# One strip loop of a deformable convolution: row terms without a spare pair, masks summed into PSUM, one bias sum for the values

## The chip, the core and the metric

The kernel runs on one core of a Trainium2 chip. The metric is the device time of one execution in microseconds. Before the change it is 2926.32 us, the median of three runs (2924.11 to 2930.4).

## What is computed

The input is 32 samples of 64 channels, 56 x 56. Two residual blocks run one after the other. The first is a pair of binary 3 x 3 group convolutions with batch norms. The second, which the change concerns, is a deformable convolution on the group-normalised sum:

```python
value = (xf @ vp_w.T + vp_b).reshape(n, L, G, cg)          # G = 8 groups of cg = 8 channels
om_in = depthwise_conv3x3(x, dw_w) + dw_b
om = om_in @ om_w.T + om_b                                 # per pixel and group: 18 offsets, 9 masks
py = row + tap_dy + off[..., 0]; px = col + tap_dx + off[..., 1]
sampled = bilinear gather of value at (py, px), zero outside the image
out = einsum('nhwgk,nhwgkc->nhwgc', mask, sampled) @ op_w.T
x = x + out
```

## The kernel before

The first block runs in passes over all samples (`l0_passes`), up to about 700 us. Then `l1_pass` handles the deformable convolution, two samples (a pair) at a time: 16 pairs, each in NT = 14 strips of BR = 4 image rows, so 224 steps. A second general path follows for offsets of a pixel or more; with these inputs it is skipped.

The gather is not done by addresses. Since offsets stay under one pixel, a bilinear sample is a product of two "hat" factors over a 5 x 5 window. For each pixel, group and tap the kernel multiplies the mask by a row hat (`mask_hats`, into `mh`) and by a column hat (`products`, into `pr`), sums the nine taps into a 5 x 5 window of weights (GpSimd `merge`, then TensorE `windows`, which shifts by columns with the matrices `smat`), and writes the weights as a band matrix through a DRAM scratch (`wst`, `w_d`) into `abuf`. TensorE multiplies this band with the values (`vbd`) in `apply`. An `apply` covers two strips (8 rows); its left and right half of the image (34 and 26 columns) go to an even and an odd step.

All engines run their own loop over the steps and meet through semaphores. Let t be the step. What each does in it, in its order:

- VectorE (`step` under `block.vector`): `copy_om(t+2)` (L960) adds the bias to the offsets and masks in PSUM `om_p` and puts them into SBUF `oms`; `mask_hats(t+1)` (L969); three `products(t+1)` (L979); in steps 0, 1, 2, 3, 5, 6 one `sum_half` and in step 7 two and the channel statistics of the next pair (L920 to L937); then `read_misc(t)`, which waits for TensorE and does `add_output` (L986) and `copy_values` (L952), in step 8 after the group statistics (L940 to L945).
- GpSimd: `merge(t+1)` (L1062, L1065), then `depthwise(t+4)`, four sums that end with L1055 and release the offsets' matmuls.
- ScalarE: `hats(t+2)` (L1119 to L1125), every second step `copy_acc`, `copy_weights(t)` (L1135, four instructions), every second step the DMA of the weights, `taps(t+5)` (L1109).
- TensorE: `apply` of an earlier strip, `windows(t)` (L1258), then one group: value rows (L1195) and offset rows for t+3 (L1200) interleaved, and the projection (L1207), whose last matmul releases `read_misc(t)`. The offset rows overwrite `om_p`, which is there once, so the group first waits for `om_ok` of tile t+2, for `dw_ok` of GpSimd, and for VectorE's last `read_misc`.
- SyncE issues the reads of `abuf` and `vbd` and the images' transfers.

The PSUM is full: `om_p`, `win_p` and `mh_p` have two banks of 512 floats each, `acc_p` and `misc` one. One row of the weights in `abuf` and `wst` has RP = 6 row terms (five and a spare), in the layout two rows x two parts, so the apply at L1280 moves whole pairs of rows (the last index, two neighbours in memory) and covers up to three pairs for each image row.

## Time and profile before

| | us |
|---|---|
| median of three runs | 2926.32 |
| the profiled execution | 2924.83 |
| its span, first to last instruction | 2923.0 |
| busy in the span: PE, DVE, ACT, POOL | 2430.8, 2205.6, 2259.7, 1917.6 |
| mean granted TensorE clock | 0.952 of full |

PE is TensorE, DVE VectorE, ACT ScalarE, POOL GpSimd; L960 is line 960. A busy time says only that an engine had an instruction running. The chain of waits of this page ends in the short flag test behind the loop and does not tell of the steps, so the reading goes by stretches, by the order of instructions in time, and by the waits.

### The profile page before, as it was taken

How to read it: one execution, taken by the hardware profiler on the slowest of the kernel's cores; microseconds unless marked ns; L12 is line 12 of the kernel's file. 1: busy time of each engine (PE TensorE's matmuls, PEld its weight loads, DVE VectorE, ACT ScalarE, POOL GpSimd, SP SyncE). 2: the span in 40 equal slices, each digit the busy share in tenths (PEclk: the TensorE clock that was granted, in tenths of full speed). 3: DMA queues.
4: the chain of work that ended last, by engine and by line, in shares of the span. 5: the costliest groups of instructions: out<-in, count | busy, mean ns of one | idle time of the engine just before them, and what ended most of it. 6: DMA issues, size and time to landing. Idle time of an engine off the chain costs nothing. (4 is left out here: it accounts for less than half of the span.)

```text
span 2923.0 us, 100581 instructions
## 1 busy us (share of the span) xinstructions
PE 2430.8 (83%) x40456; PEld 2021.2 (69%) x40456; DVE 2205.6 (75%) x3095; ACT 2259.7 (77%) x4721; POOL 1917.6 (66%) x1452
## 2 busy tenths in 40 slices
PE   3999779993688888888888888888888888888887
PEld 2666556772577777777777777777777777777786
DVE  3555423334989897989888898989898988989773
ACT  2444256662989889898989898898989898989892
POOL 1000000003888888888988888888988898988892
PEclk8999889996899999999999999999999999999998
DMA  4555579975577677777777777777778777877675
GB/s 103 130 132 144 143 182 265 263 199 172 124 191 203 181 195 192 188 191 190 204 194 192 187 200 195 197 183 193 199 189 198 188 196 187 206 179 190 177 176 147
DMA packets 356164, 538.18 MB, mean 184 GB/s; under 512 B 171728, under 2 KB 258256, under 8 KB 355536
## 3 DMA queue, kind: packets, MB, share of 16 engines
q1 hardware_dynamic: 296656, 422.71, 60.3%
q10 hardware_dynamic: 59136, 110.11, 10.8%
q8 instruction: 283, 4.64, 0.8%
q14 instruction: 89, 0.73, 0.1%
HBM read 312.82 MB, written 219.77 MB: 182 GB/s over the span
## 5 line engine op out<-in xcount | busy, mean ns | idle before, releaser
L1109 ACT ACTIVATE dwt<-xp,wts 128x224 f32<-128x224 f32 x2016 | 797.3, 484 | 40.8 <-ACT wst L1135 31.8
L1280 PE MATMUL acc_p<-abuf,vbd 128*32 128x136 f32 (+5 forms) x20480 | 710.4, 291 | 54.9 <-issue 46.0
L1280 PEld LDWEIGHTS acc_p<-abuf,vbd 128*32 128x32 f32 (+1 forms) x20480 | 645.9, 145 | 117.7 <-issue 60.5
L979 DVE TENSOR_TENSOR pr<-mh_p,ht 128x864 f32<-128x864 f32 x672 | 668.9, 1051 | 23.2
L1258 PE MATMUL win_p<-pr,smat 128*128 128x160 f32 x4032 | 626.7, 310 | 27.3 <-POOL pr L1065 15.8
L246 PE MATMUL cv<-cin,wb 128*64 128x392 bf16 x6912 | 590.4, 333 | 25.8 <-ACT cin L225 25.8
L1258 PEld LDWEIGHTS win_p<-pr,smat 128*128 128x128 f32 x4032 | 570.4, 194 | 51.2 <-issue 22.4
L246 PEld LDWEIGHTS cv<-cin,wb 128*64 128x64 bf16 x6912 | 401.4, 110 | 208.7 <-ACT cin L225 25.9
L1048 POOL TENSOR_TENSOR dwt<-dwt 128x896 f32<-128x896 f32 x224 | 516.3, 2305 | 4.7 <-ACT dwt L1109 4.7
L1062 POOL TENSOR_TENSOR pr<-pr 128x576 f32<-128x576 f32 x224 | 317.3, 1417 | 187.8 <-DVE pr L979 187.8
L1135 ACT ACTIVATE wst<-win_p 128x200 f32<-128x200 f32 x896 | 388.6, 605 | 62.4 <-PE win_p L1258 38.7
L969 DVE TENSOR_TENSOR mh_p<-oms,ht 128x864 f32<-128x864 f32 x224 | 408.8, 1825 | 8.5 <-ACT ht L1125 8.5
L1200 PE MATMUL om_p<-wts,omin 64*64 64x216 f32 x3584 | 406.4, 369 | 10.2 <-POOL omin L1055 10.2
L1195 PE MATMUL misc<-wts,xp 64*64 64x64 f32 x3584 | 181.6, 234 | 265.7 <-issue 214.3
L1195 PEld LDWEIGHTS misc<-wts,xp 64*64 64x64 f32 x3584 | 149.8, 137 | 311.2 <-issue 310.7
L1065 POOL TENSOR_TENSOR pr<-pr 128x576 f32<-128x576 f32 x224 | 338.7, 1512 | 31.2
L1050 POOL TENSOR_TENSOR dwt<-dwt 128x448 f32<-128x448 f32 x224 | 336.5, 1502 | 17.6
L1200 PEld LDWEIGHTS om_p<-wts,omin 64*64 64x64 f32 x3584 | 246.1, 139 | 47.8 <-issue 11.6
L986 DVE TENSOR_TENSOR y<-y,misc 128x224 f32 (+1 forms) x224 | 85.2, 380 | 248.2 <-PE misc L1207 247.5
L253 ACT ACTIVATE lt<-cv 128x392 f32<-128x392 f32 x128 | 60.9, 492 | 265.9 <-PE cv L246 265.5
L960 DVE TENSOR_TENSOR oms<-om_p,ombt 128x864 f32<-128x864 f32 x224 | 238.2, 1063 | 10.1 <-PE om_p L1200 10.1
L1119 ACT ACTIVATE ht<-oms 128x576 f32<-128x576 f32 x224 | 151.2, 675 | 102.7 <-DVE oms L960 102.4
(132 smaller groups left out, 2674.9 us busy)
## 6 DMA issues: line engine op xcount, KB each, us to landing
abuf<-weight_scratch SPq DMA_DIRECT2D x1568, 96.0 KB, 3.3
weight_scratch<-wst ACTq DMA_DIRECT2D x112, 960.0 KB, 6.2
xt<-x SPq DMA_DIRECT2D x128, 392.0 KB, 7.6
rows_scratch<-vsb SPq DMA_DIRECT2D x224, 128.0 KB, 2.1
vbd<-rows_scratch SPq DMA_DIRECT2D x896, 32.0 KB, 3.2
x_scratch<-xt SPq DMA_DIRECT2D x64, 392.0 KB, 6.6
y<-x SPq DMA_DIRECT2D x64, 392.0 KB, 4.4
x3h<-x_scratch SPq DMA_DIRECT2D x64, 392.0 KB, 4.9
```

Source lines behind the costliest of these rows:

```text
L246: mm = pe.matmul(cv[c][64 * h:64 * h + 64, 0:CN], wb[:, layer, j, k, :], cin[:, u, r:r + CR, k % 3:k % 3 + W], start=(k == 0 and j == 0), ...
L969: dve.tensor_tensor(mh[:, :, :, :], oms[:, j % 2, 2 * TAPS:3 * TAPS, :].unsqueeze(1).broadcast_to([LANES, 3, TAPS, BR * G]), ht[:, j % 2, ...
L979: dve.tensor_tensor(pr[:, j % 2, slots, :, :, :].rearrange("p k e x z -> p e k (x z)"), mh[:, a, :, :].rearrange("p (k x) z -> p k (x z)", ...
L1048: pool.tensor_tensor(d[:, 0:4, :], d[:, 0:4, :], d[:, 4:8, :], ALU.add).then_inc(dw1_ok, 1)
L1050: pool.tensor_tensor(d[:, 0:2, :], d[:, 0:2, :], d[:, 2:4, :], ALU.add).then_inc(dw2_ok, 1)
L1065: pool.tensor_tensor(rows(slice(1, 3)), rows(slice(1, 3)), rows(slice(5, 11, 5)), ALU.add).then_inc(mg_ok, 1)
L1109: ins = act.activation(dwt[:, j % 2, k, :].rearrange("p (r w) -> p r w", w=W), image[:, r:r + BR, k % 3:k % 3 + W], ACT.Identity, scale=dw ...
L1135: ins = act.activation(bass.AP(cells.tensor, cells.offset, [cells.ap[0], [PC, CT], [2 * BR, 2 * RT], [BAND, GS]]), win_p[:, 0:CT * WP].rea ...
L1195: return pe.matmul(misc[64 - 64 * s:128 - 64 * s, to:to + C], xp[64 * s:64 * s + 64, at:at + XL], vpw[64 * s:64 * s + 64, :], start=True, ...
L1200: return pe.matmul(om_p[64 * s:64 * s + 64, 256 * r:256 * r + OMC], omin[64 * s:64 * s + 64, j % 2, r, :], omw[64 * s:64 * s + 64, :], sta ...
L1258: mm = pe.matmul(win_p[:, to:to + 160], smat[:, e, :], pr[:, j % 2, 0:RT, a, b, :], start=n == 0, stop=n == len(terms) - 1)
L1280: mm = pe.matmul(acc_p[32 * (2 * s + b):32 * (2 * s + b) + 32, 0:2 * TN].rearrange("p (t w r) -> p t w r", t=BR, r=2)[:, t0:t1 + 1, x0:x1, :],
```

## The change

There are five parts.

1. The spare row term goes: a cell has RT = 5 rows of RW = 16 weights (PC 96 to 80 floats, a band 480 to 416 with a tail of 16, a line's read 768 to 656). The apply can then no longer move whole pairs everywhere: where a range of rows begins with an odd or ends with an even row, that row gets a matmul of its own with one element per column instead of two. A full strip goes from 12 matmuls over 48 rows to 18 over 40 for each of the four column groups.
2. The windows lie without gaps in `win_p`, so the fourth of them crosses from one bank to the next, and its matmuls are cut in two (11 instead of 9 a step, two records each).
3. `copy_weights` takes two ScalarE instructions of 400 elements instead of four of 200.
4. `copy_om` is split. `copy_offsets` writes 576 elements to `oms` in its old place. `copy_masks` writes 288 masks into the middle slot of `mh`, which lies in PSUM and is free only when the products of the tile before are done, so it stands behind the products, and `om_ok` is set there. `mask_hats` then reads its masks from PSUM: first the two outer hats (576 elements), then the middle one in place (288).
5. The values' bias is added by one instruction of 256 elements instead of two of 128; its constant is loaded once instead of twice.

```diff
@@ -58,15 +58,14 @@
 GS = 4
 CT = 5
 RT = 5
-RP = RT + 1
-WP = 172
-PC = 2 * BR * RP * 2
-BAND = CT * PC
+RW = 4 * BR
+PC = RT * RW
+BAND = CT * PC + RW
 PX = 4
-SEEN = (PX + CT - 1) * PC
+SEEN = (PX - 1) * PC + BAND
 LINE = GS * SEEN + PC
-QB = 36
-QC = 64
+QB = 37
+QC = 65
 VSLOT = 7
 TP = 2 * W
 TILES = HW // TP
@@ -947,28 +945,35 @@
                 def copy_values(i, j):
                     u = j % 2
                     wait(dve, v_out[u], 16 * turn(i, j))
-                    for h in range(2):
-                        at = TN + 2 * C * h
-                        ins = dve.tensor_tensor(
-                            vsb[:, u, :, :, 4 * h:4 * h + 4].rearrange("p g c a -> p a g c"),
-                            misc[:, at:at + 2 * C].rearrange("p (a g c) -> p a g c", g=GS, c=G),
-                            vbt[:, :, :].rearrange("p k (b g c) -> p (k b) g c", g=GS, c=G), ALU.add)
-                    return ins
-
-                def copy_om(i, j):
+                    return dve.tensor_tensor(
+                        vsb[:, u, :, :, :].rearrange("p g c (k b) -> p k b g c", b=2),
+                        misc[:, TN:TN + BR * C].rearrange("p (k b g c) -> p k b g c", k=BR, b=2, g=GS),
+                        vbt[:, :].rearrange("p (b g c) -> p b g c", b=2, g=GS).unsqueeze(1).broadcast_to([LANES, BR, 2, GS, G]), ALU.add)
+
+                def offset_sums(i, j, to, lo, hi):
+                    return dve.tensor_tensor(
+                        to.rearrange("q w (g k) -> q (w g) k", k=BR),
+                        om_p[:, :].rearrange("q (k z) -> q z k", k=BR)[:, G * lo:G * hi, :],
+                        ombt[:, G * lo:G * hi].unsqueeze(2).broadcast_to([LANES, G * (hi - lo), BR]), ALU.add)
+
+                def copy_offsets(i, j):
                     dve.wait_ge(om_ready, NT * i + j + 1)
-                    dve.tensor_tensor(
-                        oms[:, j % 2, :, :].rearrange("q w (b k g) -> q (w b) k g", b=2, g=GS),
-                        om_p[:, :].rearrange("q (k z) -> q k z", k=BR)[:, :, 0:OMC].rearrange("q k (v g) -> q v k g", g=GS),
-                        ombt[:, :].rearrange("q (v g) -> q v g", g=GS).unsqueeze(2).broadcast_to([LANES, 6 * TAPS, BR, GS]),
-                        ALU.add).then_inc(om_ok, 1)
+                    offset_sums(i, j, oms[:, j % 2, :, :], 0, 2 * TAPS).then_inc(off_ok, 1)
+
+                def copy_masks(i, j):
+                    t = NT * i + j
+                    dve.wait_ge(om_ready, t + 1)
+                    wait(dve, pr_ok, 3 * t)
+                    offset_sums(i, j, mh[:, 1, :, :], 2 * TAPS, 3 * TAPS).then_inc(om_ok, 1)
 
                 def mask_hats(i, j):
-                    wait(dve, pr_ok, 3 * (NT * i + j))
-                    dve.wait_ge(hat_ok, NT * i + j + 1)
-                    dve.tensor_tensor(mh[:, :, :, :],
-                                      oms[:, j % 2, 2 * TAPS:3 * TAPS, :].unsqueeze(1).broadcast_to([LANES, 3, TAPS, BR * G]),
-                                      ht[:, j % 2, :, 0:TAPS, :], ALU.mult).then_inc(mh_ok, 1)
+                    t = NT * i + j
+                    dve.wait_ge(om_ok, t + 1)
+                    dve.wait_ge(hat_ok, t + 1)
+                    dve.tensor_tensor(mh[:, 0:3:2, :, :], mh[:, 1, :, :].unsqueeze(1).broadcast_to([LANES, 2, TAPS, BR * G]),
+                                      ht[:, j % 2, 0:3:2, 0:TAPS, :], ALU.mult).then_inc(outer_ok, 1)
+                    dve.wait_ge(outer_ok, t + 1)
+                    dve.tensor_tensor(mh[:, 1, :, :], mh[:, 1, :, :], ht[:, j % 2, 1, 0:TAPS, :], ALU.mult).then_inc(mh_ok, 1)
 
                 def products(i, j):
 
@@ -998,11 +1003,14 @@
                 def step(i, j, first, last):
                     n = near(i, j, 2, first, last)
                     if n:
-                        copy_om(*n)
+                        copy_offsets(*n)
                     n = near(i, j, 1, first, last)
                     if n:
                         mask_hats(*n)
                         products(*n)
+                    n = near(i, j, 2, first, last)
+                    if n:
+                        copy_masks(*n)
...
@@ -1017,10 +1025,12 @@
...
                 for j in range(2):
...
-                for j in range(2):
-                    copy_om(0, j)
+                copy_offsets(0, 0)
+                copy_masks(0, 0)
+                copy_offsets(0, 1)
                 mask_hats(0, 0)
                 products(0, 0)
+                copy_masks(0, 1)
...
                     step(0, j, True, False)
...
@@ -1113,9 +1123,9 @@
 
                 def hats(i, j):
                     t, u = NT * i + j, j % 2
-                    off = oms[:, u, 0:2 * TAPS, :]
+                    off = oms[:, u, :, :]
                     wait(act, pr_ok, 3 * (t - 1))
-                    act.wait_ge(om_ok, t + 1)
+                    act.wait_ge(off_ok, t + 1)
...
                     act.wait_ge(abs_ok, t + 1)
@@ -1129,13 +1139,12 @@
                     if u == 0:
                         wait(act, w_out, 16 * (t // 2))
                     act.wait_ge(win_ok, t + 1)
-                    for k in range(BR):
-                        to = 2 * BR * (2 - 2 * (k % 2)) + BR * u + k
+                    for r in range(2):
+                        to = RW * (1 - r) + BR * u + r
                         cells = wst[:, 0, to:to + 1]
                         ins = act.activation(
-                            bass.AP(cells.tensor, cells.offset, [cells.ap[0], [PC, CT], [2 * BR, 2 * RT], [BAND, GS]]),
-                            win_p[:, 0:CT * WP].rearrange("p (e z) -> p e z", e=CT)[:, :, 0:RT * BR * G].rearrange(
-                                "p e (m k g) -> p e m k g", k=BR, g=GS)[:, :, :, k, :],
+                            bass.AP(cells.tensor, cells.offset, [cells.ap[0], [2 * BR, 2 * CT * RT], [BAND, GS], [2, 2]]),
+                            win_p[:, 0:CT * RT * BR * G].rearrange("p (m g k r) -> p r m g k", g=GS, k=2, r=2)[:, r],
                             ACT.Copy)
                     ins.then_inc(wst_ok, 1)
 
@@ -1253,11 +1262,12 @@
                     pe.wait_ge(mg_ok, t + 1)
                     for e in range(CT):
                         terms = [(a, b) for a in range(3) for b in range(3) if 2 - (a + b - 2) == e]
-                        to = WP * e
+                        cuts = (0, 1, RT) if e == 3 else (0, RT)
                         for n, (a, b) in enumerate(terms):
-                            mm = pe.matmul(win_p[:, to:to + 160], smat[:, e, :],
-                                           pr[:, j % 2, 0:RT, a, b, :],
-                                           start=n == 0, stop=n == len(terms) - 1)
+                            for m0, m1 in zip(cuts, cuts[1:]):
+                                mm = pe.matmul(win_p[:, BR * G * (RT * e + m0):BR * G * (RT * e + m1)], smat[:, e, :],
+                                               pr[:, j % 2, m0:m1, a, b, :],
+                                               start=n == 0, stop=n == len(terms) - 1)
                     mm.then_inc(win_ok, 1)
 
                 def apply(i, j, half):
@@ -1271,17 +1281,24 @@
                     qb, K, x0, x1 = ((0, 128, 0, 34), (1, 96, 30, W))[half]
                     rows = range(max(0, y0 - 2), min(H, y0 + 2 * BR + 2))
                     for yq in rows:
-                        t0, t1 = max(0, yq - y0 - 2) // 2, min(2 * BR - 1, yq - y0 + 2) // 2
-                        for s in range(S):
-                            for b in range(2):
-                                seen = abuf[0:K, s, :]
-                                at = (QB * qb + x0 - 32 * qb + 2) * PC + 4 * BR * (y0 + 2 * t0 - yq + 3) + 2 * BR * b + 2 * t0
-                                mov = bass.AP(seen.tensor, seen.offset + at, [seen.ap[0], [8 * BR + 2, t1 - t0 + 1], [PC, x1 - x0], [1, 2]])
-                                mm = pe.matmul(
-                                    acc_p[32 * (2 * s + b):32 * (2 * s + b) + 32, 0:2 * TN].rearrange("p (t w r) -> p t w r", t=BR, r=2)[:, t0:t1 + 1, x0:x1, :],
-                                    vbd[0:K, 1 - s, qb, yq // BR % VSLOT, :, :, 2 * (yq % BR) + b].rearrange("p g c -> p (g c)"),
-                                    mov, start=yq == rows[0] and qb == 0, stop=yq == rows[-1] and qb == 1,
-                                    skip_group_check=True)
+                        k0, k1 = max(0, yq - y0 - 2), min(2 * BR - 1, yq - y0 + 2)
+                        t0, t1 = (k0 + 1) // 2, (k1 + 1) // 2
+                        runs = (((k0, 1, 1),) if k0 % 2 else ()) + (((2 * t0, t1 - t0, 2),) if t1 > t0 else ()) + (
+                            ((k1, 1, 1),) if k1 % 2 == 0 else ())
+                        for ka, n, r in runs:
+                            opens = qb == 0 and yq == rows[0] and ka == k0
+                            for s in range(S):
+                                for b in range(2):
+                                    seen = abuf[0:K, s, :]
+                                    row = y0 + ka - yq + 3 - ka % 2
+                                    at = (QB * qb + x0 - 32 * qb + 2) * PC + RW * row + 2 * BR * b + ka
+                                    mov = bass.AP(seen.tensor, seen.offset + at, [seen.ap[0], [2 * RW + 2, n], [PC, x1 - x0], [1, r]])
+                                    mm = pe.matmul(
+                                        acc_p[32 * (2 * s + b):32 * (2 * s + b) + 32, 0:2 * TN].rearrange("p (t w r) -> p t w r", t=BR, r=2)[
+                                            :, ka // 2:ka // 2 + n, x0:x1, ka % 2:ka % 2 + r],
+                                        vbd[0:K, 1 - s, qb, yq // BR % VSLOT, :, :, 2 * (yq % BR) + b].rearrange("p g c -> p (g c)"),
+                                        mov, start=opens, stop=yq == rows[-1] and qb == 1 and ka == runs[-1][0],
+                                        skip_group_check=True)
                     mm.then_inc(amat_ok, 1)
 
                 def step(i, j, first, last):
```

Left out: the declarations of the buffers and semaphores, and the constant's single load.

## Rows read from the trace of the kernel before

**Rows 1.** Stretches: start:end, length, busy (instructions) per engine, clock, DMA share, GB/s
```profile
0.00:700.00 700.00, 596.66 (x6950) 408.05 (x6950) 301.30 (x662) 312.58 (x289) 39.52 (x60) 0.95 0.66 172
...
1500.00:2000.00 500.00, 417.30 (x7812) 367.39 (x7812) 446.40 (x563) 453.26 (x1033) 438.94 (x326) 0.98 0.75 194
```

**Rows 2.** Timeline of VectorE, L960 of one pair: start us, us, instruction
```profile
1548.98 1.07 DVE L960 TENSOR_TENSOR oms<-om_p,ombt 128x864 f32<-128x864 f32 x1
...
1588.35 1.05 DVE L960 TENSOR_TENSOR oms<-om_p,ombt 128x864 f32<-128x864 f32 x1
...
1595.77 1.05 DVE L960 TENSOR_TENSOR oms<-om_p,ombt 128x864 f32<-128x864 f32 x1
...
1616.76 1.05 DVE L960 TENSOR_TENSOR oms<-om_p,ombt 128x864 f32<-128x864 f32 x1
...
1631.54 1.04 DVE L960 TENSOR_TENSOR oms<-om_p,ombt 128x864 f32<-128x864 f32 x1
...
1638.13 1.06 DVE L960 TENSOR_TENSOR oms<-om_p,ombt 128x864 f32<-128x864 f32 x1
...
1682.94 1.07 DVE L960 TENSOR_TENSOR oms<-om_p,ombt 128x864 f32<-128x864 f32 x1
```

**Rows 3.** Timeline of VectorE, a step without a sum; brackets: idle before, releaser
```profile
1656.41 0.39 DVE L986 TENSOR_TENSOR y<-y,misc 128x224 f32 x1 [1.94 <-PE misc L1207]
...
1657.23 1.07 DVE L960 TENSOR_TENSOR oms<-om_p,ombt 128x864 f32<-128x864 f32 x1
1658.20 1.73 DVE L969 TENSOR_TENSOR mh_p<-oms,ht 128x864 f32<-128x864 f32 x1
1660.04 2.99 DVE L979 TENSOR_TENSOR pr<-mh_p,ht 128x864 f32<-128x864 f32 x3
```

**Rows 4.** Timeline of VectorE, step 6 with one sum
```profile
1606.82 1.10 DVE L960 TENSOR_TENSOR oms<-om_p,ombt 128x864 f32<-128x864 f32 x1
...
1612.64 1.03 DVE L920 SCALAR_TENSOR_TENSOR y<-y,ab,x3h 128x392 f32 x1
...
1616.01 0.37 DVE L986 TENSOR_TENSOR y<-y,misc 128x224 f32 x1
```

**Rows 5.** Groups of VectorE, 1000 to 2800: count | busy us, mean ns | idle before
```profile
L979 DVE TENSOR_TENSOR pr<-mh_p,ht 128x864 f32<-128x864 f32 x561 | 558.4, 1051 | 19.5
L969 DVE TENSOR_TENSOR mh_p<-oms,ht 128x864 f32<-128x864 f32 x186 | 342.2, 1840 | 0.0
```

**Rows 6.** Timeline of GpSimd, the last sum of a depthwise
```profile
1653.26 0.67 POOL L1055 TENSOR_TENSOR omin<-dwt 128x224 f32<-128x224 f32 x1
```

**Rows 7.** Timeline of TensorE, an even step's apply and windows, later an odd step
```profile
1511.27 3.42 PE L1280 MATMUL acc_p<-abuf,vbd 128*32 128x68 f32 x96
1514.62 2.71 PE L1258 MATMUL win_p<-pr,smat 128*128 128x160 f32 x18
...
1654.14 0.27 PE L1195 MATMUL misc<-wts,xp 64*64 64x64 f32 x2 [0.57 <-issue]
...
1655.67 0.59 PE L1207 MATMUL misc<-accs,wts 64*64 64x112 f32 x8
1656.19 2.80 PE L1280 MATMUL acc_p<-abuf,vbd 96*32 96x52 f32 x96
```

**Rows 8.** TensorE's waits of the whole run (us, times, longest), and an instruction queue
```profile
PE acc_p L1280 <- issue: 46.0, 41, 3.2
PE win_p L1258 <- issue: 10.7, 11, 2.2
PE acc_p L1280 <- DMA abuf<-weight_scratch: 8.6, 4, 4.4
...
q8 instruction: 283, 4.64, 0.8%
```

**Rows 9.** Timeline of a step 8: the projection, and the add that it releases
```profile
1500.46 0.69 PE L1207 MATMUL misc<-accs,wts 64*64 64x112 f32 x8
...
1502.01 0.37 DVE L986 TENSOR_TENSOR y<-y,misc 128x224 f32 x1
```

More of the change, by code:

```diff
@@ L99, in __init__ @@
         self.ombt = sb("ombt", [LANES, OMC])
[L100 removed]
+        self.vbt = sb("vbt", [LANES, C])
         self.smat = sb("smat", [128, CT, 128])
@@ L117, in load_constants @@
         sp.dma_start(self.ombt[:, :], self.omb_d).then_inc(self.con_in, 16)
-        for k in range(2):
-            sp.dma_start(self.vbt[:, k, :], self.vpb).then_inc(self.con_in, 16)
+        sp.dma_start(self.vbt[:, :], self.vpb).then_inc(self.con_in, 16)
     def clear(self, pool):
@@ L789, in l1_pass @@
         tap_ok, dw1_ok, dw2_ok, dw3_ok, dw_ok = map(sem, ("tap_ok", "dw1_ok", "dw2_ok", "dw3_ok", "dw_ok"))
-        om_ready, om_ok, abs_ok, far_ok, hat_ok, mh_ok, pr_ok, mg1_ok, mg_ok = map(sem, (
-            "om_ready", "om_ok", "abs_ok", "far_ok", "hat_ok", "mh_ok", "pr_ok", "mg1_ok", "mg_ok"))
+        om_ready, off_ok, om_ok, outer_ok, abs_ok, far_ok, hat_ok, mh_ok, pr_ok, mg1_ok, mg_ok = map(sem, (
+            "om_ready", "off_ok", "om_ok", "outer_ok", "abs_ok", "far_ok", "hat_ok", "mh_ok", "pr_ok", "mg1_ok", "mg_ok"))
         win_ok, wst_ok, amat_ok, accs_ok, misc_ready, misc_ok, carried, passed = map(sem, (
```

7 lines of the change are left out of this document (3 added, 4 removed).

## The prediction

> **What bounds the kernel now.** I read the stretch table first [rows 1]. The first 700 us are the convolution block, which the change leaves alone but for one load of constants less. From there to the end runs the second part, 224 strip steps (16 pairs of samples, 14 strips each). In it VectorE, ScalarE, GpSimd and TensorE are each busy 83 to 91% of the time. No engine alone is the bound, and the order of the waits decides.
>
> Second I read VectorE's clock over one pair: the starts of L960, its first instruction of a step, at the steps 0, 4, 5, 7, 8, 9 and the next 0 [rows 2]. Steps 0 to 3 take 39.37 us together, step 4 7.42, steps 5 and 6 20.99, step 7 14.78, step 8 6.59, steps 9 to 13 44.81: 133.96 in all. Steps 0 to 3, 5 and 6 also add one half piece of the input (`sum_half`), step 7 two; there VectorE runs without a stop, step 6 from 1606.82 to 1616.76, 9.94 us [rows 2, 4]. In a step without a sum it waits for TensorE's `misc`, 1.94 us before L986 [rows 3]; TensorE's group in turn starts 0.21 us after GpSimd's L1055 ends (1653.26 + 0.67, then 1654.14) [rows 6, 7]. So VectorE sets the pace of steps 0 to 8, GpSimd through TensorE that of 9 to 13.
>
> Third, TensorE: its offsets-and-misc group takes 2.27 us from the first matmul (1654.14) to the VectorE instruction that it releases (1656.41) [rows 3, 7]. An apply takes 3.42 us for half 0 and 2.80 for half 1, a group of windows 2.71 [rows 7].
>
> **The change, part by part.** *Masks and products on VectorE.* 864 elements with one operand in PSUM take 1.051 us (L979); `mask_hats`, as large, with both in SBUF, 1.840 [rows 5]. The change puts the masks into PSUM. Prices by size: L986 has 224 elements and takes 0.39, L979 1.051, so 1.03 ns an element and 0.16 fixed. L969 starts 0.97 us after L960 [rows 3], so what follows an instruction starts 0.08 + 1.03 ns an element after it. That makes 576 elements 0.67 to the next start and 0.75 in duration, 288 elements 0.37 and 0.45. An instruction that waits for the one before starts 0.11 after its end (L969, 1658.20 + 1.73, to L979, 1660.04) [rows 3].
> No row has a VectorE instruction that steps through PSUM 256 elements at a time, as the two new sums do, or that reads and writes one PSUM tile. Lower bound: these prices, since nothing in such an access saves work. Upper bound: the slowest row of 864 elements, 1.840, so 0.9 ns more an element, and on 1,728 elements 1.6 us a step. I take the lower end, because L960 reads PSUM in jumps already (runs of four) and costs what L979 does.
>
> *Values' bias.* From L986 to L960 pass 0.82 us [rows 3]; L986's own share is 0.30, so the two instructions of 128 elements cost 0.52. One of 256 is 0.34 by size, 0.52 if the store pattern is what costs. I take 0.42.
>
> *The release of `om_p`.* This part decides, I think. `om_ok` lets TensorE overwrite `om_p` with the next offsets. Today L960 sets it, the first work of VectorE's step. Afterwards `copy_masks` sets it, behind the products. Queued behind TensorE's wait are the value rows, the offsets, the projection, and then the next apply and windows; and VectorE's L986 of the same step waits for that projection. So a loop closes in every step: VectorE up to `copy_masks`, TensorE's group, VectorE again. Its length: L986 and the values 0.30 + 0.42; `copy_offsets` 0.67; outer hats 0.75 + 0.11; middle hats 0.45 + 0.11; products 2.99; `copy_masks` 0.11 + 0.45; to TensorE 0.21; the group 2.27. Sum 8.84 us.
> A step with a sum covers TensorE's group: 5.80 to the end of the products, 0.11 + 0.37 until the sum starts, and 3.37 from L920 to L986 (1612.64 to 1616.01) [rows 4]: 9.65 against 9.94.
> Step 8 also has the group statistics: from the projection to L986 1.55 us there, 0.74 elsewhere [rows 3, 7, 9], so 8.84 + 0.81 = 9.65.
> The pair afterwards: steps 0 to 3 38.60; step 4 8.84; steps 5 and 6 19.30; step 7 14.78 - 0.29 = 14.49; step 8 9.65; steps 9 to 13 44.20. Sum 135.08 against 133.96. The steps with sums give back 2.75 us and steps 9 to 13 0.61, but steps 4 and 8 lose 1.42 and 3.06, because today VectorE finds `misc` ready or nearly ready there. Net +1.12 a pair, x16 = +18 us.
>
> *Apply and windows on TensorE.* For each of the four column groups a full strip's apply has 12 matmuls over 48 strip rows, afterwards 18 over 40. A matmul is two records (96 for 48) [rows 7]. The halves have 34 and 26 columns, so 1,632 and 1,248 in all, for 3.42 and 2.80 us: 1.61 ns a column (both records), and 0.79 us remain for 24 passes and the tail. With 0.25 for the tail a pass costs 0.022. Afterwards: 36 x 0.022 + 0.25 + 1,360 or 1,040 x 1.61 ns = 3.23 and 2.72 us. The windows get four records more, each worth between nothing and a whole one of today, 0.15 (2.71 / 18): 0 to 0.6, I take 0.25. TensorE's round from group to group is now 2.05 to the apply (1654.14 to 1656.19), 3.35 to the windows (1511.27 to 1514.62), 2.71 for them: 8.11 with half 0, some 7.5 with half 1. It becomes 8.17 and 7.7, under 8.84 by 0.7 and 1.1.
> That cover is thin, for TensorE also stops in mid-burst for nothing that the profile names: 41 times in applies and 11 times in windows, 56.7 us, 1.1 each [rows 8]. The instruction queue meanwhile moved 283 pieces of 16.4 KB [rows 8]. If the stops are late pieces, they grow with the records: in a step of a full strip 96 in the apply and 58 elsewhere now, 144 and 62 afterwards, and denser. Bounds: no cost, and a whole stop in each of the 112 steps without a sum, 123 us. I take 0.2 us in each: +22 us.
>
> *Parts with one answer.* ScalarE's two copies instead of four come back some tenths of a microsecond, at nothing: in the step shown VectorE waits for TensorE alone [rows 3], and ScalarE works ahead of it. The weights' transfers shrink (rows of 480 to 416 and 768 to 656 elements) with as many issues on ScalarE's and SP's queues as before; the applies behind them waited 8.6 us for them in all [rows 8], so at nothing too.
>
> **Sum.** The profiled execution took 2924.83 us, its span 2923.0 and 1.8 around it; the median of the runs, 2926.32, is 0.05% above, and I correct nothing. 2924.8 + 18 + 22 = 2965 us.
>
> **The rivals.**
> *The loop is shorter than summed (faster).* L920 takes 1.03 us for 392 elements [rows 4], 0.56 by size: it stretches beside GpSimd's merge. Behind `copy_masks` it starts 0.48 later, when that merge is nearly done. If 0.15 us go in each of 8 x 16 sums, that is -19; the values at 0.34 give -18; no late TensorE: 2924.8 + 18 - 37 = 2906. Against: GpSimd only gets its turn later and holds up the next instruction. Chance 0.28.
> *No difference*, within 0.2% (6 us, about what a measurement of this kernel tells from none): half of those gains, 2924. 0.10.
> *The instructions on PSUM cost more.* A quarter of the upper bound, 0.4 us in 224 steps, is +88: 3053. Against: L960's price. 0.10.
> *TensorE becomes the bound.* The new single-row matmuls read one element in every 80, where pairs read two neighbours in every 96. If a column of theirs costs twice, 8 x 34 x 1.61 ns = 0.44 us come on top; with windows at +0.6 the round is 8.96 with half 0, over 8.84, and stops count in full: 0.7 us in 112 steps, +78: 2924.8 + 18 + 78 = 3021. Against: the pairs stream at 0.81 ns a column and record, no worse than the windows' rows without gaps (0.15 / 160, 0.94). 0.12.
> The Trainium skill (SBUF — State Buffer, section "Door 1: The DMA port swizzle", its note on cachelines) says that an access pays when it moves to a new 16-byte line each time, and that two hits a line are wanted. By it the single rows are the bad case and the pairs the good one; this trace has pairs alone, so it does not show the rule either way.
>
> **How the numbers follow.** My case 0.40, at 2965 (2940 to 2990). Faster 0.28, same 0.10, slower 0.40 + 0.10 + 0.12 = 0.62. The range 2895 to 3050 reaches from the faster rival to the two slow ones and leaves out the dearer half of the PSUM bound and a loop still shorter.
>
> **What would show it.** In every step without a sum VectorE should wait some 2.5 us before L986's successor, ended by TensorE, and TensorE's group should be released by `copy_masks` in nearly every step. Steps 4 and 8 should be longer, the steps with sums shorter by about 0.3. The hats should read 0.75 and 0.45 us. Stops within applies should be more numerous. The prediction is wrong if steps 9 to 13 fall well under 8.8 us each, or if TensorE's group is ready by the time that VectorE wants it.

## The result, and the profile after

The changed kernel takes 3102.64 us (median; 3087.4 to 3111.84) against 2925.22 us: ratio 1.060, 95% interval 1.055 to 1.066, so 177 us slower. Slower was forecast, by 40 us; the time lies outside the range given. The profiled execution took 3087.4 us, its span 3085.6.

The first stretch is the same; in the second part VectorE, ScalarE and GpSimd fell from 88 to 91% busy to some 75% [rows 1]. Stretches of the changed kernel (columns as in [rows 1]):

```profile
0.00:700.00 700.00, 597.06 (x6950) 413.89 (x6950) 300.88 (x664) 312.56 (x289) 40.01 (x60) 0.95 0.66 172
1500.00:2000.00 500.00, 414.43 (x9496) 374.50 (x9498) 379.23 (x572) 381.35 (x846) 368.99 (x294) 0.94 0.58 163
```

TensorE has 9,496 matmul records there instead of 7,812 and is no busier; its granted clock is 0.94 instead of 0.98. Groups of VectorE in the changed kernel, 1000 to 2900 us (L948 is the values' bias, L954 the two sums, L973 and L976 the hats, L984 the products):

```profile
L984 DVE TENSOR_TENSOR pr<-mh_p,ht 128x864 f32<-128x864 f32 x546 | 543.7, 1052 | 18.9
...
L954 DVE TENSOR_TENSOR oms<-om_p,ombt 128x576 f32<-128x576 f32 x182 | 141.1, 775 | 0.0
...
L973 DVE TENSOR_TENSOR mh_p<-mh_p,ht 128x576 f32<-128x576 f32 x182 | 136.9, 752 | 0.0
L948 DVE TENSOR_TENSOR vsb<-misc,vbt 128x256 f32<-128x256 f32 x182 | 128.2, 704 | 0.0
...
L976 DVE TENSOR_TENSOR mh_p<-mh_p,ht 128x288 f32<-128x288 f32 x182 | 85.0, 467 | 6.3
L954 DVE TENSOR_TENSOR mh_p<-om_p,ombt 128x288 f32<-128x288 f32 x181 | 84.5, 467 | 6.2
```

VectorE's prices came out as forecast, but for the values' bias: 0.70 us long, and 0.52 to the start of the next instruction (median), where 0.42 was forecast. What grew are the waits. VectorE's wait for `misc` in the kernel before, then waits of the changed kernel, over the whole run (us in all, times, longest):

```profile
DVE y L986 <- PE misc L1207: 247.5, 109, 10.9
```

```profile
DVE y L991 <- PE misc L1216: 479.3, 142, 10.7
...
PE acc_p L1296 <- issue: 217.0, 118, 4.2
...
PE misc L1204 <- DVE mh_p L954: 126.3, 105, 5.1
...
PE win_p L1268 <- issue: 22.3, 17, 3.2
```

and of its page, the queue of instruction pieces:

```profile
q8 instruction: 374, 6.13, 0.8%
```

VectorE waits for `misc` nearly twice as long as before. TensorE's stops in the middle of an apply, which the profile puts down to nothing, went from 46.0 [rows 8] to 217.0 us, and it now waits for `copy_masks` 105 times. Both can be seen in two neighbouring steps. TensorE, changed kernel (start us, us, instruction, in brackets the idle time before):

```profile
1714.33 0.27 PE L1204 MATMUL misc<-wts,xp 64*64 64x64 f32 x2 [1.26 <-DVE mh_p L954]
...
1716.38 2.52 PE L1296 MATMUL acc_p<-abuf,vbd 128*32 128x34 f32 x99
1720.57 1.24 PE L1296 MATMUL acc_p<-abuf,vbd 128*32 128x136 f32 x45 [1.67 <-issue]
1721.74 3.06 PE L1268 MATMUL win_p<-pr,smat 128*128 128x160 f32 x22
1724.73 0.27 PE L1204 MATMUL misc<-wts,xp 64*64 64x64 f32 x2
...
1726.78 2.93 PE L1296 MATMUL acc_p<-abuf,vbd 96*32 96x26 f32 x144
```

and VectorE in the same stretch:

```profile
1716.60 0.39 DVE L991 TENSOR_TENSOR y<-y,misc 128x224 f32 x1 [2.53 <-PE misc L1216]
1716.90 0.73 DVE L948 TENSOR_TENSOR vsb<-misc,vbt 128x256 f32<-128x256 f32 x1
1717.44 0.79 DVE L954 TENSOR_TENSOR oms<-om_p,ombt 128x576 f32<-128x576 f32 x1
...
1719.50 2.99 DVE L984 TENSOR_TENSOR pr<-mh_p,ht 128x864 f32<-128x864 f32 x3
1722.52 0.47 DVE L954 TENSOR_TENSOR mh_p<-om_p,ombt 128x288 f32<-128x288 f32 x1
1727.00 0.39 DVE L991 TENSOR_TENSOR y<-y,misc 128x224 f32 x1 [4.01 <-PE misc L1216]
```

The first group (1714.33) waited for `copy_masks`, as forecast, and VectorE for the projection, 2.53 us. In its apply TensorE stops for 1.67 us after 99 of 144 records; so the next group starts at 1724.73, 1.74 us after `copy_masks` had ended (1722.99), and VectorE waits 4.01 us. The step took 10.4 us.

From the starts of VectorE's first sum in each step (`copy_om` before, the 576 elements of L954 after) I worked out the steps' lengths, apart by how many half pieces of input they add:

| step, us | forecast | before | after | e1 (below) | e2 (below) |
|---|---|---|---|---|---|
| no sum: shortest tenth / median / mean | 8.84 | 6.60 / 8.58 / 8.61 | 8.88 / 9.53 / 10.12 | 8.86 / 8.91 / 9.44 | 6.62 / 9.15 / 9.22 |
| one sum: median / mean | 9.65 | 9.94 / 10.05 | 9.19 / 10.09 | 9.12 / 9.35 | 9.92 / 9.99 |
| step 7, two sums: median | 14.49 | 14.80 | 14.03 | 15.60 | 14.78 |

A pair has 7, 6 and 1 of these. By the means the loss is all in the steps without a sum: 7 x (10.12 - 8.61) x 16 = 169 us. Step by step it is less simple: of the 14 steps of a pair, steps 0, 4, 8 and 12 lose 2.7, 3.9, 3.9 and 1.8 us on the mean, and the other ten together gain 1.1. Step 0 has a sum; it is among the losers, and the steps 1, 2, 3 and 5 that gain hide it in the table. The shortest tenth before, 6.60 us, is step 8 (median 6.33).

### The profile page after: what moved, and what is told of

Its sections match the earlier page's. It is cut to its first block and busy times, and to the rows that moved or that the text cites. A ratio compares the mean times of both kernels' runs of the same rounds, so it can differ in the third digit from the quotient of the medians.

```text
span 3085.6 us, 123708 instructions
## 1 busy us (share of the span) xinstructions
PE 2568.7 (83%) x52104; PEld 2190.5 (71%) x52104; DVE 2060.7 (67%) x3319; ACT 2114.6 (69%) x4273; POOL 1776.5 (58%) x1452
## 5 line engine op out<-in xcount | busy, mean ns | idle before, releaser
L1296 PE MATMUL acc_p<-abuf,vbd 128*32 128x34 f32 (+5 forms) x31232 | 737.6, 252 | 222.9 <-issue 217.0
L1296 PEld LDWEIGHTS acc_p<-abuf,vbd 128*32 128x32 f32 (+1 forms) x31232 | 687.7, 155 | 276.1 <-issue 239.2
L1268 PE MATMUL win_p<-pr,smat 128*128 128x160 f32 (+2 forms) x4928 | 768.0, 316 | 22.3 <-issue 22.3
L1268 PEld LDWEIGHTS win_p<-pr,smat 128*128 128x128 f32 x4928 | 710.8, 209 | 39.3 <-issue 27.0
L984 DVE TENSOR_TENSOR pr<-mh_p,ht 128x864 f32<-128x864 f32 x672 | 669.1, 1052 | 23.5 <-DVE mh_p L976 0.5
L1058 POOL TENSOR_TENSOR dwt<-dwt 128x896 f32<-128x896 f32 x224 | 509.2, 2273 | 4.7 <-ACT dwt L1119 4.7
L1145 ACT ACTIVATE wst<-win_p 128x400 f32<-128x400 f32 x448 | 216.7, 543 | 363.9 <-PE win_p L1268 356.8
L1209 PE MATMUL om_p<-wts,omin 64*64 64x216 f32 x3584 | 392.5, 360 | 20.2 <-DVE mh_p L954 13.2
L1060 POOL TENSOR_TENSOR dwt<-dwt 128x448 f32<-128x448 f32 x224 | 263.0, 1174 | 17.6
L921 DVE SCALAR_TENSOR_TENSOR y<-l2h,ab,y 128x392 f32 (+1 forms) x128 | 198.6, 1551 | 4.5
```

Source lines behind the costliest of these rows:

```text
L984: dve.tensor_tensor(pr[:, j % 2, slots, :, :, :].rearrange("p k e x z -> p e k (x z)"), mh[:, a, :, :].rearrange("p (k x) z -> p k (x z)", ...
L1058: pool.tensor_tensor(d[:, 0:4, :], d[:, 0:4, :], d[:, 4:8, :], ALU.add).then_inc(dw1_ok, 1)
L1060: pool.tensor_tensor(d[:, 0:2, :], d[:, 0:2, :], d[:, 2:4, :], ALU.add).then_inc(dw2_ok, 1)
L1145: ins = act.activation(bass.AP(cells.tensor, cells.offset, [cells.ap[0], [2 * BR, 2 * CT * RT], [BAND, GS], [2, 2]]), win_p[:, 0:CT * RT * ...
L1209: return pe.matmul(om_p[64 * s:64 * s + 64, 256 * r:256 * r + OMC], omin[64 * s:64 * s + 64, j % 2, r, :], omw[64 * s:64 * s + 64, :], sta ...
L1268: mm = pe.matmul(win_p[:, BR * G * (RT * e + m0):BR * G * (RT * e + m1)], smat[:, e, :], pr[:, j % 2, m0:m1, a, b, :], start=n == 0, stop= ...
```

## The experiments

For each kernel I measured two things of TensorE in its trace. Its *work* in a step is the step's mean length less its mean wait between the windows and the next group (1000 to 2880 us). The *excess* is what applies and windows took beyond the tenth percentile of bursts of their kind, summed from 760 to 2880 us: stops, and whatever runs slower around them. In a slower kernel fewer steps lie in that stretch; to the end of the run the excess is 110 us before, 374 after, 282 in e2, 449 in e3 and 497 in e9.

| kernel | time, us | ratio [95%] | release of `om_p` | apply, shortest tenth, half 0 / 1, us | instructions in it | pieces | work + wait in a step, us | excess, us |
|---|---|---|---|---|---|---|---|---|
| before | 2925 | | early | 3.39 / 2.76 | 192 | 283 | 8.49 + 1.13 | 107 |
| after | 3103 | 1.060 [1.055, 1.066] | late | 3.30 / 2.90 | 288 | 374 | 9.96 + 0.51 | 349 |
| e1 | 2964 | 1.014 [1.011, 1.018] | late | 3.38 / 2.76 | 192 | 283 | 8.42 + 1.40 | 115 |
| e2 | 2985 | 1.021 [1.018, 1.024] | early | 3.29 / 2.90 | 288 | 374 | 9.50 + 0.43 | 274 |
| e3 | 3120 | 1.067 [1.063, 1.070] | early | 4.02 / 3.56 | 384 | 443 | 10.47 + 0.03 | 400 |
| e4 | 2934 | 1.003 [1.002, 1.004] | early | 5.03 / 3.94 | 192 | 283 | 9.25 + 0.44 | 17 |
| e5 | 3095 | 1.057 [1.054, 1.060] | late | 3.31 / 2.90 | 288 | 367 | 9.77 + 0.71 | 384 |
| e6 | 2958 | 1.013 [1.009, 1.018] | late | 5.02 / 3.96 | 192 | 283 | 9.36 + 0.44 | 23 |
| e7 | 2922 | 0.998 [0.997, 1.000] | early | 3.38 / 2.75 | 192 | 283 | 8.57 + 1.07 | 103 |
| e8 | 3079 | 1.052 [1.048, 1.056] | early | 5.38 / 4.44 | 384 | 443 | 10.37 + 0.00 | 180 |
| e9 | 3226 | 1.103 [1.099, 1.107] | late | 4.55 / 3.56 | 384 | 443 | 10.91 + 0.16 | 426 |
| e10 | 3004 | 1.027 [1.025, 1.029] | late | 5.03 / 3.98 | 192 | 290 | 9.81 + 0.18 | 11 |
| e11 | 3078 | 1.053 [1.051, 1.056] | late | 3.30 / 2.90 | 288 | 374 | 10.02 + 0.41 | 360 |

(Instructions: matmul records and as many weight loads. Pieces: those of queue q8 in the whole run. In e9 most applies stop, so its shortest tenth of 4.55 us for half 0 is not free of stops, and its excess is too small.)

**e1: the late release alone.** Before, with VectorE's part of the change, which also has the hats on PSUM and the one sum for the values. The cut of the code is simplified, its comments are added.

```diff
-    copy_om(*n)                    # 864 elements, frees om_p at the start of the step
+    copy_offsets(*n)               # 576 elements into oms
     mask_hats(*n); products(*n)
+    copy_masks(*n)                 # 288 elements into mh[:, 1], om_ok set here
```

> The kernel before with VectorE's half of the change alone: masks summed into the PSUM tile behind the products (the late release of om_p) and the values' bias in one instruction; apply, windows and ScalarE's copies stay, so TensorE's program stays. Theory 'TensorE's instruction stream' (the matmul records added by the apply and windows make TensorE stop in mid-burst, and that carries the loss): stops inside TensorE's bursts stay at about 54 with 75 us, time 2925 to 2945 (my sum for the late release alone was +18). Rival 'late release' (VectorE and TensorE in lockstep carry the loss): 3050 to 3100, with VectorE waiting for misc 480 us in all as in the changed kernel. Rival 'interaction' (either half alone is covered): under 2960, and e2 under 2960 too.

Measured 2964 us, +38: more than the first theory allowed, far less than the "late release" rival, and not under 2960. Its waits:

```profile
DVE y L992 <- PE misc L1218: 329.4, 115, 11.6
PE misc L1206 <- DVE mh_p L955: 320.2, 184, 7.5
...
DVE g L939 <- PE misc L1200: 70.1, 16, 5.1
...
PE acc_p L1291 <- issue: 46.7, 29, 3.5
```

TensorE's group is released by `copy_masks` in 184 steps, and the step without a sum has its median at 8.91 us where 8.84 was summed. The loop is there as described, and its own price is 38 us, not 177. Step 8 takes 11.5 us (median), 1.9 more than forecast: once a pair VectorE waits 4.4 us for the matmul of the group statistics (L939), for which it waited 1.5 us in all before. Step 7 is long here because it also waits for a transfer (`l2h`, 26.8 us in 14 waits; 4.6 in the changed kernel).

**e2: all but the late release.** After (simplified cut), with one sum of 864 elements into SBUF at the start of the step, and the old `mask_hats`.

```diff
-    copy_offsets(*n)
+    copy_om(*n)                    # offset_sums over 0..3*TAPS into oms, om_ok set here
     mask_hats(*n); products(*n)    # masks read from oms, one product of 864 elements
-    copy_masks(*n)
```

> The changed kernel with the early release: all 864 offsets and masks are summed into SBUF by one instruction at the start of VectorE's step, which frees om_p, and the masks are multiplied with the hats by one instruction as in the kernel before; the five row terms, ScalarE's two copies, the windows and the values' bias stay as changed. Theory 'TensorE's instruction stream': stops as in the changed kernel, about 135 with 280 us, time 3040 to 3110. Rival 'late release': 2905 to 2940, no slower than before. Rival 'interaction': 2925 to 2985, because TensorE's stops fall where VectorE no longer waits.

Measured 2985 us, +59: less than the first theory, at the upper end of the "interaction" rival. Its waits:

```profile
DVE y L983 <- PE misc L1203: 330.9, 113, 8.9
...
PE acc_p L1283 <- issue: 161.5, 95, 3.7
...
PE misc L1191 <- issue: 93.5, 75, 3.0
```

The stops are there without the late release (161.5 us in applies). 38 and 59 make 97 of the 177 us: some 80 come only where both meet.

**e3: more records, nothing else.** Before, each matmul of the apply cut in two by columns.

```diff
+    for xa, xb in ((x0, (x0 + x1) // 2), ((x0 + x1) // 2, x1)):
         for s in range(S):
             for b in range(2):
-                mm = pe.matmul(..., [PC, x1 - x0], ...)
+                mm = pe.matmul(..., [PC, xb - xa], ...)
```

> The kernel before with each matmul of the apply cut in two by columns: as many columns and the same access patterns, but 192 records instead of 96 in an apply (144 in the changed kernel); VectorE, ScalarE and the release of om_p stay. An apply gets longer by 24 passes of 0.022 us, 0.5 us, when nothing stops. Theory 'TensorE's instruction stream': more than 135 stops in mid-burst and over 280 us, time 3050 to 3250. Rival 'late release': no more than the 0.5 us in a round with slack: 2925 to 2985. Rival 'single rows' (what costs in the changed kernel is the single-element step of the new matmuls): 2925 to 2985 as well, stops as before.

Measured 3120 us. From its page, the applies and the queue of pieces:

```profile
q8 instruction: 443, 7.26, 1.1%
...
L1281 PE MATMUL acc_p<-abuf,vbd 128*32 128x102 f32 (+4 forms) x40960 | 872.9, 241 | 278.1 <-issue 274.1
```

Records alone, without a changed access pattern or a moved wait, bring the stops, as the first theory said: 274.1 us where there were 46.0 [rows 8]. The time is not the stops' alone, since an apply also takes 0.6 to 0.8 us longer where nothing stops.

**e4: five row terms without more records.** Before, each image row in a slot of its own, so that one matmul reads its rows with a single-element step; 12 matmuls a column group stay, over 40 rows instead of 48. ScalarE copies the windows in two instructions, by planes.

```diff
-PC = 2 * BR * RP * 2
+PC = RT * 4 * BR
-    mov = bass.AP(..., [seen.ap[0], [8 * BR + 2, t1 - t0 + 1], [PC, x1 - x0], [1, 2]])
+    mov = bass.AP(..., [seen.ap[0], [4 * BR + 1, k1 - k0 + 1], [PC, x1 - x0]])
```

> The kernel before with five row terms in another form: every image row of a strip has a slot of its own, so that an apply keeps 12 matmuls for each column group (96 records) but over 40 rows instead of 48, each row read with a single-element step; ScalarE copies the windows in two instructions (output planes 0 to 2 and 3 to 4) instead of four; windows keep 18 records; masks, hats and values as before. Theory 'TensorE's instruction stream': records are as before, so stops stay at 54 with 75 us, and 8 x 34 columns less are 0.44 us less in each apply of half 0: 2880 to 2925. Rival 'single rows' (a column read with a single-element step costs twice): an apply of half 0 takes 5.2 us instead of 3.42, TensorE is the bound in every step: 3050 to 3150. Rival 'late release': 2900 to 2930.

Measured 2934 us. The page's line on its applies, and two bursts of its timeline:

```profile
L1278 PE MATMUL acc_p<-abuf,vbd 128*32 128x170 f32 (+9 forms) x20480 | 997.7, 363 | 3.1 <-issue 2.4
```

```profile
1515.38 5.06 PE L1278 MATMUL acc_p<-abuf,vbd 128*32 128x34 f32 x96
1520.36 2.71 PE L1256 MATMUL win_p<-pr,smat 128*128 128x160 f32 x18
```

The rival's price is right: less 0.53 for 24 passes and 0.25 for the tail, 1,360 columns take 4.3 us of the 5.06, 3.1 ns each against 1.61 for pairs. Its time is wrong, and so is the first theory's, which left the stops as they were: TensorE works 0.76 us more a step than before, and the kernel is 0.3% slower. With 283 pieces as before, the stops in applies are 2.4 us instead of 46.0: at the same number of instructions they went when each took longer (5.03 us / 192 = 26 ns instead of 18).

**e5: windows whole again.** After, the fourth plane moved to the second bank of its PSUM tile, four ScalarE copies.

```diff
-    cuts = (0, 1, RT) if e == 3 else (0, RT)
+    to = WAT[e]                    # (0, 160, 320, 512, 672)
```

> The changed kernel with windows whole again: the fourth of the five planes starts at the second bank of the PSUM tile, so none is cut; windows go back from 22 to 18 records (3.06 to 2.71 us undisturbed), ScalarE copies in four instructions of 160 to 240 elements instead of two of 400; applies, masks and the late release stay as changed. Theory 'stops in the applies carry the loss': 0.35 us less a step, of which about two thirds reach the end, 3040 to 3070, with the apply's mean (5.1 and 3.7 us) unchanged. Rival 'the windows' cut carries it' (its records and the stops inside windows, 0.83 us a step against the kernel before): under 3000.

Measured 3095 us. That is above the 3040 to 3070 expected, and no different from the changed kernel within the spread of its runs (3087 to 3112). The windows' four records more cost next to nothing; the applies still stop, and the loss stays:

```profile
PE acc_p L1297 <- issue: 239.1, 121, 5.1
```

**e6: late release, hardly any stops.** e4 with VectorE's part of the change.

> e4 (uniform rows, in which TensorE's stops were nearly gone: 10 with 14 us) with the late release of e1 (masks summed into the PSUM tile behind the products, values' bias in one instruction). If the late release costs by its own loop (my step): as much as in e1, 2965 to 2985. If it costs only where TensorE's stops fall into the loop: 2925 to 2945.

Measured 2958 us, between the two expectations: 25 us over e4. Its waits:

```profile
DVE y L992 <- PE misc L1216: 340.9, 137, 6.7
...
PE misc L1204 <- DVE mh_p L955: 112.2, 93, 5.1
```

With e1 this prices the late release, with the rest of VectorE's part, where stops are few: 25 to 38 us.

**e9: late release, many stops.** e3 with VectorE's part of the change.

> e3 (each matmul of the apply cut in two, +193 us, TensorE busy without a wait for others: 0.03 us a step) together with the late release of e1 (+38 us). If the two add up: 3155 to 3165. If the late release is hidden, because TensorE doesn't wait for anyone in e3: 3115 to 3140. If stops and late release strengthen each other as in the changed kernel (the stops cost 51 us with the early release, 2934 to 2985, and 145 with the late one, 2958 to 3103): 3190 or more.

Measured 3226 us, 107 over e3, as the third expectation had it. Its waits:

```profile
DVE y L992 <- PE misc L1218: 616.6, 163, 8.6
...
PE acc_p L1292 <- issue: 341.3, 181, 5.1
```

So the late release costs 25 (e4 to e6) and 38 us (before to e1) where the excess is 17 to 115 us, and 117 (e2 to after) and 107 us (e3 to e9) where it is 274 to 426. The two strengthen each other, in two different layouts of the apply.

**e10: as much TensorE work, but even.** e6, the second plane of the windows computed twice, first in vain.

```diff
-    for e in range(CT):
+    for e in (1, *range(CT)):
```

> e6 (late release, uniform rows, hardly any stops; TensorE works 9.36 us a step and waits 0.44) with the second plane of the windows computed twice, first in vain: 0.60 us more in every step, always the same, at a low density of instructions. TensorE's work in a step is then 9.96 us, as in the changed kernel (9.95). If only the mean of TensorE's work matters, a step takes 10.47 us as there: 3085 to 3110. If it is the unevenness of the stops (none in most steps, 2 to 4 us in some, which the next wait cannot give back): 10.0 to 10.2 us a step, 3000 to 3045.

Measured 3004 us, in the second range; TensorE's work in a step is 9.81 us. Two bursts of its timeline:

```profile
1516.58 5.09 PE L1289 MATMUL acc_p<-abuf,vbd 128*32 128x34 f32 x96
1521.60 3.26 PE L1267 MATMUL win_p<-pr,smat 128*128 128x160 f32 x22
```

With nearly the changed kernel's mean work (9.96) and the same late release, but 11 us of excess instead of 349, it is 99 us faster. The mean costs as well: e10 is 45 us slower than e6, for 0.45 us more work a step. So of the 144 us from e6 to the changed kernel 45 come with the mean work of e10, at most 34 (0.15 x 224) with the work that the changed kernel has beyond it, and the rest, at least 65, with the unevenness, as far as the two layouts of the apply are otherwise alike.

**e8: density or length.** e4, its matmuls cut in two by columns as in e3.

> e4 with each matmul of the apply cut in two by columns, as e3 did it to the kernel before: TensorE's program is as long as in e3 (443 pieces), but each record takes longer, since its columns cost twice: 384 records and weight loads in some 5.5 us, 14.4 ns each, against 10.3 in e3 (where there were 199 stops), 14.4 to 17.8 in the kernel before (57) and 26 in e4 (10). Theory 'density' (stops come when TensorE runs through a piece of 256 instructions faster than the next can come): some 40 to 90 stops, as in the kernel before, windows undisturbed. Rival 'length' (stops go with the number of pieces): 150 or more, as in e3. The time is that of a TensorE that is the bound: 2934 + 0.5 x 224 = 3045 by density, 3150 and more by length.

Measured 3079 us, excess 180, some 105 stops (as the expectation counts them, over 0.45 us from one matmul's start to the next).

```profile
PE acc_p L1279 <- issue: 117.4, 99, 3.3
```

Neither: more than the density theory allowed, half of what length alone gave (e3, 443 pieces as well: 400). By halves: half 0 (5.38 us / 384 = 14.0 ns an instruction) takes 1.2 us more on the mean than in the shortest tenth, half 1 of before (2.76 us / 192 = 14.4 ns) 0.36. So the number in a row counts, not the speed alone. Nor do the two decide together: half 1 of e8 has as many instructions, runs them faster (4.44 us / 384 = 11.6 ns), and takes only 0.50 us more.

**e7 and e11: the values' bias in the order of its store.** One instruction that writes neighbours and reads PSUM in steps of 64 elements, in the kernel before (e7) and after (e11, whose edit is shown, shortened; in e7 it replaces the two instructions).

```diff
-    vsb[...].rearrange("p g c (k b) -> p k b g c", b=2), misc[...] as "p k b g c"
+    vsb[...].rearrange("p g c (k b) -> p (g c) k b", b=2), misc[...] as "p z k b"
```

> The kernel before with one thing changed: the values' bias is added by one VectorE instruction of 256 elements that runs in the order in which it stores (neighbours in SBUF, steps of 64 elements in PSUM). In the changed kernel the one instruction ran in PSUM's order and took 0.70 us, the two of before 0.86 together. Theory 'the store pattern is what costs' (reads from PSUM in wide steps cost nothing extra, as the sums of 576 and 288 elements showed): 0.42 us by size, 0.44 less in each step; where VectorE sets the pace (steps 0 to 8, 9 x 16 = 144) that is -63 us, in all 224 steps -98: 2830 to 2880. Rival 'either order costs the same': 0.70 us, 2890 to 2926. Rival 'TensorE's loop hides it': 0.42 us but 2910 to 2930.

> The changed kernel with the values' bias in the order of its store, 0.42 us instead of 0.70 (e7). In the kernel before the 0.44 us saved so gave 5 us in all. If VectorE and TensorE run in lockstep in the changed kernel, with the values on the loop, 0.29 us are saved in each of 224 steps: 3035 to 3055. If TensorE alone sets the pace there: 3095 to 3105.

e7's group of VectorE, 1000 to 2900 us:

```profile
L950 DVE TENSOR_TENSOR vsb<-misc,vbt 128x256 f32<-128x256 f32 x195 | 81.3, 417 | 0.0
```

It takes the forecast 0.42 us, yet e7 is only 5 us faster than before, as its third expectation had it: VectorE waits for `misc` longer instead (291.5 us against 247.5). The saving is also smaller than expected, since the two instructions of before overlapped: from the start of the values to the next instruction 0.33 us instead of 0.50, not 0.44 less. e7 is faster than before by 0.2%, at the edge of what a measurement tells. In the changed kernel the instruction is 0.29 us shorter, and the next one starts 0.19 sooner; that gives 25 us (3078, between the two expectations), 0.11 a step, so VectorE seems to lie on the loop in part of the steps, not in all.

## Why the prediction was right or wrong

**Right: the loop.** `copy_masks` releases TensorE's group, in 184 steps of e1 and in 105 of the changed kernel (nearly every one of 224 was forecast), and VectorE's wait is 2.53 us where some 2.5 were forecast. Without stops a step of the loop takes 8.9 us (8.84 forecast). Steps with a sum came out shorter, 9.1 to 9.2 instead of 9.65, as the "shorter" rival had foreseen, though not by how much: L920 (median 1.04 us) ran beside the first of the two sums of GpSimd's merge, L918, its successor, runs beside the second and takes 0.62. Step 8 came out longer, 11.5 us in e1 instead of 9.65, by the wait for the group statistics, which the sum did not have. Alone the release costs 25 to 38 us (+18 forecast).

**Right: the prices on VectorE and of the undisturbed bursts.** 0.78, 0.47, 0.75 and 0.47 us for sums and hats; an apply at 3.30 and 2.90 us (3.23 and 2.72 forecast), windows 3.06 (2.71 + 0.25 forecast). The rival "instructions on PSUM cost more" falls.

**Wrong: the stops, the term of +22.** The step "I take 0.2 us in each" of 112 steps, with an upper bound of 123. Measured, TensorE's and ScalarE's part of the change costs 59 us with the early release (e2) and 138 with the late one (e1 to the changed kernel), and the excess went from 107 to 349 us. The term also counted only the steps without a sum, while those with one have a median of 9.19 us and a mean of 10.09. The stops are late instruction pieces as far as the trace can tell, which the prediction had named: in the changed kernel there are some 135 stops over 0.45 us, and more than eight in ten of them end 1.26 to 1.53 us after a piece of queue q8 has landed. Pieces come some 6 us apart, so by chance about one in twenty would. A piece is 256 instructions: the changed kernel has 23,296 matmul records and weight loads more than the one before, and 91 pieces more. Pieces hardly ever came closer together than 3.4 us (one interval in a hundred). An undisturbed apply of half 0 ran through 256 instructions in 3.39 / 192 x 256 = 4.5 us before; it does so in 3.30 / 288 x 256 = 2.9 us now. I scaled the stops with the number of records, when they rise far more where TensorE runs through its instructions faster than pieces follow. The 192 and 288 instructions with the burst's time and the smallest interval between pieces (3.6 us before) would have pointed at it beforehand.

The Trainium skill (Runtime: NRT & Kernel Launch, section "Instruction fetch mechanics") describes the refill in blocks of 256 instructions while the current one executes, and says that crossing a block is "mostly hidden", since instructions are dispatched more slowly than blocks arrive. The trace agrees with the blocks and not with the hiding: 10 to 11.5 ns an instruction in the undisturbed applies of the changed kernel, against 13 ns in the closest pieces (3.4 us / 256).

Speed does not explain all of it. Half 1 runs through its instructions faster than half 0 in every kernel, and yet in the changed kernel it is stopped less: 36 of 101 applies stop, 1.5 us each, against 64 of 101 and 2.3 us. There the DMA engines are busy 0.50 of the first 3 us of a half 1 and 0.91 of those of a half 0 (142 and 302 GB/s). Whether the data transfers hold up the pieces was not tested: no run kept the instructions and moved the transfers.

**Wrong: a stop was priced by its length, and by the cover it has in one step.** Two things make it dearer. First the clock. Stretches of TensorE in the changed kernel around one stop (columns as in [rows 1]), and its timeline:

```profile
1690.85:1694.06 3.21, 3.21 (x136) 3.07 (x135) 3.14 (x5) 3.14 (x9) 2.91 (x4) 1.00 1.04 346
1694.06:1696.44 2.38, 0.01 (x2) 0.00 (x0) 2.24 (x7) 0.00 (x0) 0.74 (x1) 1.00 0.57 117
1696.44:1701.50 5.06, 5.05 (x32) 4.74 (x31) 4.84 (x10) 3.06 (x6) 0.00 (x0) 0.66 0.42 113
```

```profile
1690.85 3.21 PE L1296 MATMUL acc_p<-abuf,vbd 128*32 128x34 f32 x134
1696.44 0.40 PE L1296 MATMUL acc_p<-abuf,vbd 128*32 128x68 f32 x10 [2.38 <-issue]
1696.77 4.73 PE L1268 MATMUL win_p<-pr,smat 128*128 128x160 f32 x22
```

TensorE had worked at the full clock, stood still for 2.38 us, and the granted clock of the next 5 us is 0.66, part of them at the lower of its two levels: the windows take 4.73 us instead of 3.06. Of the thirty longest stops in the changed kernel 28 are followed by such a drop within 5 us. From 760 to 2880 us, 52 bursts of its windows touch a stretch at the lower level (11 before), and 79 of the 94 us of the windows' excess lie in them.

Second, the late release leaves less room to catch up. Of the 77 steps 9 to 13, 24 are under 8.5 us with the stops and the early release (e2; 14 before, none in e4, which hardly stops). With the late release none is under 8.8, with many stops or few (changed kernel, e1, e6, e9, e10), because the loop is as long as that. The short steps 4 and 8 of the kernel before (medians 7.44 and 6.33) are another matter: e4 has them too, at 7.47 and 6.32, so they do not come from catching up, and their loss was in the forecast. e2, with 167 us more excess than the kernel before, takes 59 us more time, and the changed kernel, with 234 us more than e1, takes 138.

The forecast had both terms and added them. Measured, they are 38 and 59 us, and some 80 more come where both meet, which the sum put at nothing. e1, e2, e3, e6 and e9 show that the two strengthen each other. That this goes by the lost room alone is not shown: the late release also makes the excess itself larger.

**Wrong, with little weight: the values' bias.** The forecast reckoned to the start of the next instruction, 0.42 us with bounds 0.34 and 0.52; it is 0.52, the bound for a costly store pattern, and no less than the two instructions took (0.50). e7 shows that the order of the store was what cost (0.33). e11 prices it at 25 us in the changed kernel.

**The rivals.** Nearest came "TensorE becomes the bound" (3021): stops in full, but in the steps without a sum alone and without the clock. Its price of a single row is borne out by e4, 3.1 ns a column with one element a line against 1.61 with two neighbours; so is the Trainium skill's rule behind it (SBUF — State Buffer, section "Door 1: The DMA port swizzle", the note on cachelines). In the changed kernel the price did not come up: an undisturbed half 0 took 3.30 us, not the 3.67 that twice the price makes of 3.23, and a record of 34 single-row columns took 16.4 ns from start to start on the mean, one of 34 columns in pairs 16.1 (e3).

**Open:** why the late release itself makes stops more (274 to 349 us, 400 to 426; to the end of the run 282 to 374 and 449 to 497), and what decides which of the pieces come late; the traffic of the data transfers is a candidate. Nothing here changed how pieces are fetched; that they cause the stops rests on the times of their landing and on e3, e4 and e8.

## What to carry to other kernels

Before cutting a TensorE burst into more and shorter instructions, divide its time by its instructions, weight loads included, and compare that with the time of an instruction piece; a burst that comes near that time is at risk of stops, whatever the columns say (here 13 ns an instruction; e8 stopped at 14 as well). Before moving a release behind other work, look for the shortest steps as well as the mean: a loop whose floor rises towards the mean has little room to catch up after an uneven neighbour. Two such risks that are small when taken singly should be priced together.

## What the runs showed of the hardware

- Instruction pieces of TensorE (16 KB, 256 instructions): hardly ever closer than 3.4 us in the changed kernel and 3.7 before; a stopped engine goes on some 1.4 us after the piece landed.
- A stop of 2.4 us in mid-burst was followed by a granted clock of 0.66 over 5 us, and the burst behind it took 4.73 us instead of 3.06.
- VectorE: sums that step through PSUM 256 elements at a time, and products that read and write one PSUM tile, take 0.75 to 0.78 us for 576 elements and 0.47 for 288, as by size. A sum of 256 elements from PSUM that stores to SBUF out of order takes 0.70 us; stored in order it takes 0.42, while reading PSUM in steps of 64 (e7).
- An fp32 matmul whose moving rows are read one element at a time costs 3.1 ns a column for both records where a matmul has up to five rows (e4), pairs of neighbours 1.61. A matmul of one single row of 34 columns costs no more than one of 17 pairs, 16.4 and 16.1 ns a record (changed kernel, e3).
